# Part of layer 1's product with adj computed during layer 0: 44 of 256 strips, with buffers moved to make room

## The reference, cut to what matters

```
L0: XW = f(x @ W0);  r = rowscale(adj @ [gamma*XW, gamma-1], adj row sums);  x1 = LN(x + r)
L1: deg = rowsum(adj + I);  d = deg**-0.5
    x2 = LN(x1 + (d * ((adj + I) @ (d * x1))) @ W1.T + b1)
L2: adj_norm @ x2 and a masked attention softmax(beta * cos(x2, x2) * adj) @ x2;  x3 = LN(...)
L3: agg = adj @ x3, a GRU cell on it;  x4 = LN(x3 + ...)
```

## Time and profile before

| | |
|---|---|
| median of 3 runs | 1423.76 us (1414.07 to 1426.44) |
| the profiled execution | 1423.67 us, its span 1421.9 us |
| granted TensorE clock over the span | 0.974 |
| busy in the span | PE 1312.5, PEld 1018.2, DVE 1084.8, ACT 1059.4, POOL 577.8 us |
| layer 0's multiplies | 39.2 to 420.5 us |
| layer 1's multiplies | 422.7 to 645.2 us |
| layers 2 and 3 | to 1155 and to 1421.9 us |

### The profile page before, as it was taken

How to read it: one execution, slowest core, us unless ns; L and a number is a source line. 1 busy time by engine, 2 the same in 40 slices (tenths; PEclk the granted TensorE clock), 3 DMA queues, 4 the chain that set the end, 5 groups by cost and what they waited for, 6 DMA issues and landing times.

```text
span 1421.9 us, 21055 instructions
## 1 busy us (share of the span) xinstructions
PE 1312.5 (92%) x7640; PEld 1018.2 (72%) x7640; DVE 1084.8 (76%) x1943; ACT 1059.4 (75%) x1369; POOL 577.8 (41%) x441
## 2 busy tenths in 40 slices
PE   5999999999988989998899999999999879999995
PEld 5999999999976767773466666666665658666663
DVE  6855556555668989998888887988888878777874
ACT  6887887788777667775688878788797557667663
POOL 4312222222454533343377767777776640000010
PEclk9899999999999999999899999999999999999998
DMA  9999999999957868894688778787786849877850
GB/s 306 377 387 331 357 359 353 339 357 360 339 222 256 321 242 323 328 373 160 238 274 308 267 269 314 271 297 290 245 320 204 281 172 422 325 267 264 297 183 22
DMA packets 114808, 413.08 MB, mean 291 GB/s; under 512 B 10000, under 2 KB 23568, under 8 KB 90128
## 3 DMA queue, kind: packets, MB, share of 16 engines
q1 hardware_dynamic: 106256, 407.54, 79.0%
q10 hardware_dynamic: 8448, 4.20, 1.0%
HBM read 340.40 MB, written 71.30 MB: 290 GB/s over the span
## 4 chain that ended last, share of the span: by engine, by line
PE 52%; DVE 19%; ACT 16%; issue 7%; POOL 5%; DMA 1%; POOLq 0%; ACTq 0%; DVEq 0%; SPq 0%
DVE part_l L1346 6%; PE strip_b L596 5%; PE acc L541 5%; PE acc L532 4%; PE acc L533 4%; PE acc L513 3%; PE mid L513 3%; ACT arena L755 3%; DVE part_l L1225 3%; PE acc L613 3%; PE acc L610 2%; PE acc L611 2%; PE strip_b L493 2%; ACT part_h L810 2%; ACT part_h L762 2%
## 5 line engine op out<-in xcount | busy, mean ns | idle before, releaser
L1346 DVE TENSOR_TENSOR part_l<-arena,part_h 128x1024 fp32r<-128x1024 f32 x256 | 327.0, 1313 | 60.6 <-ACT part_h L810 59.4
L1059 POOL TENSOR_TENSOR part_l<-arena,part_h 128x512 fp32r<-128x512 f32 x237 | 304.4, 1298 | 152.2 <-ACT part_h L848 152.2
L810 ACT ACTIVATE part_h<-arena 128x1024 fp32r<-128x1024 f32 x256 | 265.4, 1055 | 125.9 <-PE acc L541 113.0
L1225 DVE TENSOR_TENSOR part_l<-arena,part_h 128x1024 fp32r<-128x1024 f32 x128 | 161.0, 1266 | 124.2 <-ACT part_h L762 123.6
L848 ACT ACTIVATE part_h<-arena 128x512 fp32r<-128x512 f32 x256 | 157.7, 623 | 95.3 <-DVE arena L1428 94.7
L532 PE MATMUL acc<-part_h,Y 128*128 128x512 f32 x512 | 220.5, 431 | 5.5 <-ACT part_h L810 3.0
L533 PE MATMUL acc<-part_h,Y 128*128 128x512 f32 x512 | 203.8, 398 | 0.0
L1027 POOL TENSOR_TENSOR sc<-sc,power 128x4 f32<-128x4 f32 x32 | 49.4, 1543 | 330.0 <-DVE sc L1251 330.0
L596 PEld LDWEIGHTS strip_b<-ident,arena 128*128 128x128 f32 x1024 | 126.8, 142 | 69.2 <-DVE arena L1428 19.6
L541 PE MATMUL acc<-part_l,Y 128*128 128x512 f32 x512 | 164.5, 403 | 10.1 <-DVE part_l L1346 9.7
L596 PE MATMUL strip_b<-ident,arena 128*128 128x128 f32 x1024 | 156.6, 276 | 15.7 <-DVE arena L1428 11.2
(11 more groups left out here) (258 smaller groups left out, 2786.8 us busy)
## 6 DMA issues: line engine op xcount, KB each, us to landing
arena<-adj_t SPq DMA_DIRECT2D x128, 1024.0 KB, 4.9
arena<-in_adj SPq DMA_DIRECT2D x64, 1024.0 KB, 8.2
adj_t<-arena SPq DMA_DIRECT2D x64, 1024.0 KB, 7.6
arena<-in_adj SPq DMA_DIRECT2D x128, 512.0 KB, 5.9
part_h<-adj_t SPq DMA_DIRECT2D x64, 512.0 KB, 5.1
part_l<-adj_t SPq DMA_DIRECT2D x64, 512.0 KB, 5.2
scratch<-v ACTq DMA_DIRECT2D x8, 256.0 KB, 10.2
arena<-scratch SPq DMA_DIRECT2D x8, 256.0 KB, 5.2
```

What stands on the lines that cost most here:

```text
L810: act.activation(flat(part_h[:, slot:slot + 2, :]), turned_pair(n), ACT.Copy).then_inc(high_done, 1)
L1059: pool.tensor_tensor(part_l[:, b % 4, :], mixed[b % G_SLOTS], part_h[:, b % 4, :].bitcast(F32), ALU.subtract).then_inc(low_done, 1)
L1225: dve.tensor_tensor(flat(part_l[:, slot:slot + 2, :]), full_pair(n), flat(part_h[:, slot:slot + 2, :]).bitcast(F32), ALU.subtract).then_in ...
L1346: dve.tensor_tensor(flat(part_l[:, slot:slot + 2, :]), turned_pair(n), flat(part_h[:, slot:slot + 2, :]).bitcast(F32), ALU.subtract).then_ ...
```

## The change

Layer 1's product is linear in the blocks, so blocks whose inputs are known early can be multiplied while layer 0 still holds their parts. Once layer 0 has finished slabs 0 and 1 of rows, d * x1 of groups 0 and 1 is known. With `FUSED = 2`, layer 0 multiplies group 0 for layer 1 in slab 2, and groups 0 and 1 in slabs 3 to 7: 11 groups, 22 steps, 44 strips. Layer 1 leaves these steps out, 106 steps remain.

- Y gets a layout in planes: high half, low half, and a third plane with the high half of layer 1's inputs (`y1_high`) beside `y1_low`. In a fused step each couple of matmuls becomes three: `part_l` by two planes (260 columns, not adjacent), `part_h` by three planes (390 columns), `part_h` by `y1_low` (128 columns). In all other steps of layer 0 the 260 columns of `part_h` are now two planes that are not adjacent.
- Slabs from 2 on take the groups in the order 0, 2, 3, 4, 1, 5, 6, 7, so fused steps are the 1st, 2nd, 9th and 10th of a slab. Slabs 0 and 1 of layer 1 take them in nearly that order.
- After a slab, `read_acc0` is two `tensor_reduce` on DVE alone, which add the two halves on the way (POOL's `sum_parts` and `sum_den` go). ACT reads the partial sums of layer 1 (`read_partial`), SP stores them (`put_partial`, 256 KB) and loads them back in layer 1 into `turned` (`load_partial`); POOL adds them to the identity's share (`add_partial`), which now covers slabs 2 to 7.
- The bias is added to x in place by POOL right behind `eye_share`, and `x_bias` leaves the chain of row steps.
- To make room, `mx` lies in `x_nat`, and x is loaded again in layer 0's slab 1 (two DMAs of 1 MB). The fp16 halves of the unit vectors are made in `v` and moved by a DMA issued on ACT after row step 14 (`units_in`); the first scores wait for it.

```diff
+                both = g < fused(s)
                 for j in (2 * m, 2 * m + 1):
...
+                        if both:
+                            if start:
+                                pe.matmul(sums, h, planes[:, :, j, :], start=True, stop=False)
+                            pe.matmul(sums[:, 0:3:2, :], low, planes[:, 0:3:2, j, :], start=False, stop=False)
+                            if not start:
+                                pe.matmul(sums, h, planes[:, :, j, :], start=False, stop=False)
+                            last = pe.matmul(sums[:, 2, 0:D], h, y1_low[:, j, :], start=False, stop=False)
+                        else:
+                            if start:
+                                pe.matmul(sums[:, 0:2, :], h, Y[:, :, j, :], start=True, stop=False)
+                            last = pe.matmul(sums[:, 0, :], low, Y[:, 0, j, :], start=False, stop=False)
+                            if not start:
+                                last = pe.matmul(sums[:, 0:2, :], h, Y[:, :, j, :], start=False, stop=stop)
...
             def read_acc0(s):
+
                 dve.wait_ge(product, slab_product(0, s))
...
+                for n in range(2):
+                    parts = both0(n)[:, :, 0:2 * LO].rearrange("p q (h w) -> p q w h", w=LO)
+                    if n == 1 and s >= 2:
+                        dve.wait_ge(partial_half, s - 1)
+                    dve.tensor_reduce(sums_of[s % 2][:, 2 * n:2 * n + 2, :], parts, AX.X, ALU.add
+                                      ).then_inc([sums_half, acc_read][n], 1)
...
+            def read_partial(s):
+
                 act.wait_ge(product, slab_product(0, s))
+                if s >= 4:
+                    act.wait_ge(partial_out[s % 2], partials_at(s - 2))
+
+                act.activation(partial(s)[:, 2:4, :], both0(1)[:, :, 2 * LO:2 * LO + D], ACT.Copy).then_inc(partial_half, 1)
+                act.wait_ge(sums_half, s + 1)
+                act.activation(partial(s)[:, 0:2, :], both0(0)[:, :, 2 * LO:2 * LO + D], ACT.Copy).then_inc(partial_read, 1)
...
+                made, count = (eye_in, s + 1) if s < 2 else (eye_scaled, s - 1)
+                pool.tensor_tensor(by_block(eye[s % 2]), x_nat[:, mine, :], wide(dcol[:, mine]), ALU.mult).then_inc(made, 1)
+
+                pool.wait_ge(made, count)
+                pool.tensor_tensor(x_nat[:, mine, :], x_nat[:, mine, :],
+                                   bias1[:].unsqueeze(1).to_broadcast([P, Q, D]), ALU.add).then_inc(biased, 1)
+
+            def add_partial(s):
+                pool.wait_ge(eye_scaled, s - 1)
+                pool.wait_ge(partial_in[s % 2], partials_at(s))
+                pool.tensor_tensor(eye[s % 2], eye[s % 2], turned[s % 2][:], ALU.add).then_inc(eye_in, 1)
...
+                if k == 15:
+                    act.wait_ge(row[s % 2], row_done(1, s, "unit_low"))
+                    if s == 0:
+                        act.wait_ge(product, product_base[1])
+                    act.dma_start(halves_of[:, s, :, :].bitcast(F32), unit_new[s % 2]).then_inc(units_in[s % 2], 16)
```

More of the change, by code:

```diff
@@ L22 @@
 PAIRS = NB // 2
-YW = 2 * D + 4
 LO = D + 2
@@ L315, in groups_loaded @@
         def groups_loaded(l, n):
-            before = sum(i % TURNED_SLOTS == n % TURNED_SLOTS for i in range(GROUPS * SLABS)) if l == 3 else 0
+            before = sum(i % TURNED_SLOTS == n % TURNED_SLOTS for i in range(STEPS1 // 2)) if l == 3 else 0
             return 16 * (before + n // TURNED_SLOTS + 1)
@@ L507, in multiply0 @@
                     for q in range(Q):
-                        mine = slice(P * q, P * (q + 1))
-                        if start:
-                            pe.matmul(acc0[q][:, 0:YW], part_h[:, slot, mine], Y[:, j, :], start=True, stop=False)
-                        last = pe.matmul(acc0[q][:, 0:LO], part_l[:, slot, mine], Y[:, j, 0:LO], start=False, stop=False)
-                        if not start:
-                            last = pe.matmul(acc0[q][:, 0:YW], part_h[:, slot, mine], Y[:, j, :], start=False, stop=stop)
+                        h, low = [part[:, slot, P * q:P * (q + 1)] for part in (part_h, part_l)]
+                        sums = acc0[q][:, 0:3 * LO].rearrange("p (h w) -> p h w", w=LO)
+                        if both:
[11 more added lines that the diff above has]
+                                last = pe.matmul(sums[:, 0:2, :], h, Y[:, :, j, :], start=False, stop=stop)
                 last.then_inc(product, 1)
             def multiply(l, n):
-                s, m = TURNS[n]
+                s, m = TURNS[l][n]
+                first = 2 * fused(s) if l == 1 else 0
                 to = acc[:, s % 2, :]
@@ L668, in _ @@
                 multiply0(n)
-            for n in range(TURNS_ALL):
+            for n in range(STEPS1):
                 for k, s in hooks(1, n):
@@ L1044, in before @@
                     pool.wait_ge(row[par], row_before(1, s, name))
-                if k == 0:
-                    before("x_bias")
-                    pool.tensor_tensor(v[:], x_nat[:, mine, :],
-                                       bias1[:].unsqueeze(1).to_broadcast([P, Q, D]), ALU.add).then_inc(row[par], 1)
                 if k == 5:
@@ L1109, in _ @@
                         eye_share(s)
+                    if n == ROWS_FROM[1][s] - 3 and s >= 2:
+                        add_partial(s)
             for n in range(STEPS2):
```

344 lines of the change are left out of this document (221 added, 123 removed).

## The result

| | before | after |
|---|---|---|
| median on the same chips | 1420.08 us (1412.66 to 1426.60, 20 runs) | 1427.48 us (1420.52 to 1432.66, 20 runs) |
| profiled execution, span | 1423.67, 1421.9 us | 1425.49, 1423.7 us |
| granted TensorE clock | 0.974 | 0.979 |

The ratio is 1.0056, 95% interval 1.0043 to 1.0069: the change costs 0.56% (7.4 us) where I forecast 0.6% less time. The time is inside my range; the sign is wrong.

What follows compares the result with a forecast made beforehand. PE was taken to bound layer 0, PE and DVE together layer 1. Terms 32.2 - 12.4 + 3.5 + 1 - 28.3 - 8 + 1.8 + 2 = -8.2 took 1423.67 us to 1415.5, range 1398 to 1430.

Steps and rivals of the forecast that it cites:

- Layer 1's steps: -28.3: Layer 1, removed steps: four fewer per slab bring 25.6 us to 20.5, saving 28.3 us in all.
- the -34.5 of layer 1: Layer 1: the prediction's terms for this layer taken together, 34.5 us saved.
- The bias leaves the chain: -8: Layer 1: PE no longer waits 5.11 us for x_bias in POOL's queue; 8 us saved, bounds 0 and 9.3.
- Fused steps: +32.2: Layer 0: each of 22 fused steps costs 1.46 us more, 32.2 us added, bounds 30.8 and 41.
- What the fused steps hide: -12.4: Layer 0, slabs 3 to 7: extra PE work fills the wait on ACT (7.3) and keeps the clock up (5.1).
- End of a slab: +3.5: Layer 0, slab ends: DVE's two reductions keep PE waiting longer, 0.5 x 7 = 3.5 us, bounds 0 and 7.
- Copies, reloads and waits: +1: Layer 0: reloads of x behind a store and y1_parts waiting for POOL add 1 us, bounds 0 and 5.
- The last inputs: +1.8: POOL's queue: eye_share(0) and the bias ahead of y_low(7) delay PE by 1.8 us, bounds 0 and 4.
- Between layers 1 and 2: +2: Layer 1 to 2: later turn_unit and waiting for the units' 256 KB DMA add 2 us, bounds 0 and 6.
- The first rival: Nothing is hidden in layer 0 (+12.4), or the bias wait only moves (+8): 1424 to 1428 us, chance 0.20.

Runs made afterwards that it cites:

- e7: Kernel before, with the bias added to x in place behind eye_share and x_bias out of the chain: 1417.19 us, ratio 0.9979 (0.9957 to 1.0002).
- e8: Changed kernel with add_partial two steps earlier, y1_parts moved into the next slab, and eye_share(0) moved behind y_low(7): one execution, 1418.58 us.
- e5: Changed kernel without the third matmul (128 columns) of each fused triple: one execution, 1411.01 us.
- e6: Kernel before, with only Y laid out in two planes, so wide matmuls read two runs: one execution, 1419.25 us beside 1417.09 before.

## Why the prediction was wrong, step by step

- **The step that failed** is "Layer 1's steps: -28.3". It took PE's work and DVE's work out of a slab and let the 0.6 us idle time stand. It looked for the queue of `load_partial` (SP) and not for that of `add_partial` (POOL), which stands behind `unit`, which waits for ACT's rows. My own list of what would make the forecast wrong has "a new wait (for partials) before PE"; none of the rivals gave it a price. The prediction itself had read this queue in the kernel before, where `x_bias` stood behind the same `unit`. Measured: 2.0 of the 3.3 us that each such slab is over 20.5, and 8 us of layer 1 (the medians differ by 14). A period runs from ACT's copy of one slab's sums to the next copy. In these the -34.5 of layer 1 were 1.0 up to slab 2's copy, 13.1 in slab 2's period with the bias, 15.3 in the three behind it and 5.1 in the last; the trace gives 1.8, 4.5, 5.2 and 4.8. What failed lies in the four periods in which PE waits for the addition.
- **The rest of that step**, 20.5 for what is 21.8, is inside its bounds (19.4 to 22). The addition's price for DVE at 0.4 was low: each POOL operation can hold a DVE operation for its whole length, as the Trainium skill's page SBUF — State Buffer, section SBUF: two separate sides, has it, but taking that away gave nothing back.
- **"The bias leaves the chain: -8"**: the mechanism is right, the size is not. Alone it is -5.3. What was late next was not `unit` but ACT's copy of the sums behind the rows of slab 1, a wait of 2.25 us in e7 and of 3.28 in the changed kernel, there at 1.2 GHz again (2.05 us for `times_w`, as before).
- **"Fused steps: +32.2"** held. Ordinary and fused steps of PE in layer 0, start to start:

```profile
228.25 1.03 PE L585 MATMUL strip_b<-ident,arena 128*128 128x128 f32 x8
...
231.00 1.04 PE L585 MATMUL strip_a<-ident,arena 128*128 128x128 f32 x8
...
262.07 1.03 PE L585 MATMUL strip_a<-ident,arena 128*128 128x128 f32 x8
...
266.22 1.04 PE L585 MATMUL strip_b<-ident,arena 128*128 128x128 f32 x8
```

  4.15 - 2.75 is 1.40 where I had 1.46: 30.8 for 22. The floor for short matmuls, 0.10, measured 0.106.
- **"What the fused steps hide: -12.4"** was low. In slab 4 the first of the late fused steps starts at 262.07 and the next at 266.22, with no wait ahead of either. Four fused steps add 5.6 us and the end of the slab about 0.5, the slabs went from 48.3, 46.7 and 48.3 (mean 47.8) to 50.4: 3.5 hidden per slab and not 2.5. Beside the 1.65 us the smaller waits for ACT in the slab went, and the clock stayed at 2.4 GHz as I had expected.
- **"End of a slab: +3.5"** held: PE waits 0.57 us at 238.09, DVE's reductions took 0.70 and 0.69 where I had 0.69.

```profile
238.09 0.42 PE L610 MATMUL acc<-inputs,part_h 128*128 128x390 f32 x1 [0.57 <-DVE sums L1404]
```

- **"Copies, reloads and waits: +1"** was low, and so was its bound of 5, since I gave `y1_parts` no price: ACT waits for POOL's `y_scale`, PE for ACT, and the clock falls. Slabs 2 and 3 took 5.5 and 4.3 us more than before, 9.8 in all. Their six fused steps (8.4), the two ends (1.0) and what such steps hide (3.5 as in the later slabs and, I estimate, half of it where there are two) make 4.2 of it, so some 5.6 are left. Step by step the trace has most of it: the steps with PE's two waits took 4.54 and 4.52 us where they had 2.74, so 3.6, and the one behind the first 4.37, so 1.6 for the clock; it fell there and not behind the second.

```profile
126.25 0.63 ACT L874 ACTIVATE inputs<-turned 128x512 fp32r<-128x512 f32 x1 [4.29 <-POOL turned L1124]
```

```profile
127.93 1.48 PE L585 MATMUL strip_a<-ident,arena 128*128 128x128 f32 x7 [1.63 <-ACT arena L883]
```

- **"The last inputs: +1.8"**: no such cost (e8). **"Between layers 1 and 2: +2"**: the rest of the span grew by 1.8, but layer 2 ends 0.6 earlier than before, and the loss stands in layer 3 (267.2 us against 264.8), whose work is that of before and which took 261.3 us in e7; no wait of PE for the units' DMA stands in the trace.

The range held because its bounds for unknown costs were wide, and that was luck. The first rival has the right size (1424 to 1428) by another way: its first half, nothing hidden in layer 0, is refuted by the 3.5 us a slab, its second, that the bias wait only moves, came true in part (3.28 us for 5.11), and it doesn't name the queue of `add_partial`, the loss that two steps took away.

## What to carry to other kernels

When work is handed to an engine that is half idle, write down what stands in front of it in that engine's queue and what that waits for; busy time says nothing of it. Give an operation that another engine needs a place in front of the calls that wait for late chains, and check this again for each length of the loop: an offset from the end that is right for 12 steps was wrong for 14. If a change removes the steps of one layer, each row step that was placed by counting them has moved against the rest.

## What the runs showed of the hardware

- A VectorE operation on four columns takes 0.15 to 0.17 us, or 1.0 to 1.2 when a GpSimd operation of 512 columns is running as it starts, and ends with it. GpSimd pays too: one addition of 512 columns took 1.28 us there and 2.24 beside `low`.
- fp32r matmuls with a weight load each: 0.106 us with 128 columns (e5), 0.233 with 512, both at 2.4 GHz.
- A moving operand in two runs, 4,160 elements apart (32 blocks of 130; the expectation of e6 says 4,224), costs PE 0.02 to 0.03 us in a step of eight such matmuls; one in three runs (390 columns) costs 0.18 us (a fused triple of 0.42 less 0.13 and 0.106), as on the line between one run of 260 and one of 512.
